# A threshold search of a sparse layer: level and count in one tile, one predicated copy per bracket end, both masks from one instruction, the level as a ninth candidate, no negated level

## The reference, cut to what matters

```python
z = x_flat @ ternary_quant(W_syn).T + b_syn          # [2048, 1024]
k = max(1, int(N * (1.0 - TARGET_SPARSITY)))         # 102
topv, _ = jax.lax.top_k(z, k)
thresh = topv[:, -1:]                                # the 102nd largest of each token
hidden = jnp.where(z >= thresh, jax.nn.relu(z), 0.0)
out = hidden @ ternary_quant(W_out).T + b_out
return layernorm(x + out, gamma, beta)
```

## Time and profile before

| | |
|---|---|
| time, median of 3 runs | 1194.39 us (1192.79 to 1199.39) |
| time of the profiled execution | 1195.06 us |
| its span, first to last instruction | 1193.3 us |
| busy in the span | PE 91%, PEld 62%, DVE 76%, ACT 52%, POOL 18% |
| granted TensorE clock, mean | 0.962 |

### The profile page before, as it was taken

One profiled execution on the slowest core, in us unless ns is written; L12 is line 12 of the kernel. 1 busy time (PEld: TensorE's weight loads), 2 busy tenths in 40 slices (PEclk: granted clock), 3 DMA queues, 4 the chain that ended last, 5 costly groups with the idle time before them and its releaser, 6 DMA issues. The chain is left out here.

```text
span 1193.3 us, 18401 instructions
## 1 busy us (share of the span) xinstructions
PE 1084.1 (91%) x7046; PEld 745.7 (62%) x7046; DVE 904.9 (76%) x1698; ACT 625.9 (52%) x1096; POOL 216.0 (18%) x176
## 2 busy tenths in 40 slices
PE   8889999999999989777867889999997899999998
PEld 8623333333333437566757768888886698989976
DVE  7689999999999634689888886555553878798853
ACT  5338787887887764776641233333333433433343
POOL 1308100000000002000034203000000744554410
...
GB/s 198 235 133 55 17 40 54 24 34 55 31 26 2 2 1 32 1 1 1 11 9 1 1 93 33 21 36 19 36 1 50 14 1 1 1 1 1 1 67 5
DMA packets 25290, 40.02 MB, mean 34 GB/s; under 512 B 3560, under 2 KB 12784, under 8 KB 25200
## 3 DMA queue, kind: packets, MB, share of 16 engines
...
...
q10 hardware_dynamic: 576, 0.00, 0.0%
...
## 5 line engine op out<-in xcount | busy, mean ns | idle before, releaser
L771 DVE TENSOR_REDUCE att_mx<-att_ps_m 128x2 f32<-128x1024 f32 x256 | 310.9, 1224 | 23.6 <-PE att_ps_m L637 19.9
L748 ACT ACTIVATE att_prob<-att_ps_s 128x512 f32<-128x512 f32 x512 | 278.2, 596 | 88.5 <-PE att_ps_s L687 76.5
L703 PE MATMUL att_ps_o<-att_prob,v_rows 128*32 128x256 f32 (+1 forms) x1920 | 159.3, 405 | 0.0
L1980 POOL TENSOR_TENSOR qry_prod<-qry_qr,lin_ksum 128x512 f32<-128x512 f32 x64 | 92.9, 1451 | 303.7 <-ACT qry_qr L2102 289.6
L687 PE MATMUL att_ps_s<-qst,kst 50*128 50x512 f32 x512 | 128.0, 496 | 11.0 <-ACT att_prob L748 10.4
L687 PEld LDWEIGHTS att_ps_s<-qst,kst 50*128 50x128 f32 x512 | 48.0, 183 | 123.8 <-ACT att_prob L748 114.2
L637 PE MATMUL att_ps_m<-kst,qst 48*128 48x512 f32 x512 | 109.9, 424 | 8.8 <-DVE att_mx L771 7.2
L2102 ACT ACTIVATE qry_qr<-qry_ps_q 128x512 f32<-128x512 f32 x64 | 38.3, 598 | 132.8 <-PE qry_ps_q L153 124.0
L153 PE MATMUL qry_ps_o<-qry_m,qry_n_hi 128*128 128x256 f32 x512 | 99.5, 293 | 0.5 <-DVE qry_n_lo L2010 0.5
L703 PEld LDWEIGHTS att_ps_o<-att_prob,v_rows 128*32 128x32 f32 x1920 | 38.1, 108 | 84.7 <-ACT att_prob L748 71.1
L1692 DVE SCALAR_TENSOR_TENSOR key_k_lo<-kf_ps,key_k_hi 128x512 fp32r<-128x512 f32 x64 | 44.2, 691 | 61.6 <-ACT key_k_hi L1770 61.0
...
## 6 DMA issues: line engine op xcount, KB each, us to landing
...
```

The costliest lines, as they stand in the source:

```text
L703: ins = nc.tensor.matmul(ps_o[32 * h:32 * h + 32, cols], vall[:, NS * b + s, h0 + h, :], prob[:, u % PR, h, cols], start=s == 0, stop=s == ...
L748: nc.scalar.activation(prob[:, u % PR, 2 * j + r, :], ps_s[:, (n + r) % BANKS, :], ACT.Exp).then_inc(exp_ok, 1)
L771: nc.vector.reduce_max(mx[:, v % 2, :, m], ps_m[:, n % 2], AX.X).then_inc(m_rd, 1)
L1980: nc.gpsimd.tensor_tensor(prod[:, u % 2, :], qr[:, u % 2, :], ksum[:, b, cols(n)], ALU.mult).then_inc(pr_ok, 1)
```

## The change

`lev` and `cnt` become the two halves of one tile `now`, and the four bracket arrays become one tile `ends` (side, level or count, tile), so that one predicated copy of 128x8 moves a level and its count. Both masks come out of one `scalar_tensor_tensor` against a constant tile `below_end` of ones and zeros. `square` and `missed` lose their waits. The two bracket widths are one subtraction. The Sign activation gets scale -1 and the level itself as bias, so `nlev` goes, in `first_level` too. The bracket's first ends are computed from mean and deviation and not from the level. In `threshold` the level is put in front of the eight as a ninth candidate, the counts are compared with a constant tile `place`, and the flag is reduced first. `settle` writes the integer flag in one instruction. On POOL there are two more small memsets at the start of the stage, on DVE one more instruction on `place` in step 0.

```diff
--- before.py
+++ after.py
@@ -879,21 +879,23 @@
...
-        lev = st.sb("lev", [P, d.NT])
-        nlev = st.sb("nlev", [P, d.NT])
+        now = st.sb("now", [P, d.NC, 2, TPC])
         sgn = st.sb("sgn", [P, d.NT])
-        cnt = st.sb("cnt", [P, d.NT])
-        lo, hi, clo, chi = (st.sb(n, [P, d.NT]) for n in ("lo", "hi", "clo", "chi"))
+        ends = st.sb("ends", [P, 2, 2, TPC])
+        width = st.sb("width", [P, 2, TPC])
+        below_end = st.sb("below_end", [P, 2, TPC])
         missed = st.sb("missed", [P, d.NT])
-        t1, t2, t3, msk = (st.sb(n, [P, TPC]) for n in ("t1", "t2", "t3", "msk"))
+        t1, t2, t3 = (st.sb(n, [P, TPC]) for n in ("t1", "t2", "t3"))
+        msk = st.sb("msk", [P, 2, TPC])
+        doubt = st.sb("doubt", [P, 2 * TPC])
...
-        top = st.sb("top", [P, d.NT, 8])
-        pick = st.sb("pick", [P, TPC, 8])
-        iota8 = st.sb("iota8", [P, 8])
-        iota_i = st.sb("iota_i", [P, 8], mybir.dt.int32)
+        top = st.sb("top", [P, d.NT, 9])
+        pick = st.sb("pick", [P, TPC, 9])
+        place = st.sb("place", [P, 9])
+        iota_i = st.sb("iota_i", [P, 9], mybir.dt.int32)
         thr = st.sb("thr", [P, d.NT])
         flag = st.sb("flag", [P, 2])
         flag_i = st.sb("flag_i", [P, 1], mybir.dt.int32)
@@ -963,7 +965,9 @@
             def _(pool):
                 link = chain(pool, gp)
                 link(nc.gpsimd.memset(ones[:], 1.0))
-                link(nc.gpsimd.iota(iota_i[:], pattern=[[1, 8]], base=0, channel_multiplier=0))
+                link(nc.gpsimd.iota(iota_i[:], pattern=[[1, 9]], base=0, channel_multiplier=0))
+                link(nc.gpsimd.memset(below_end[:, 0, :], 1.0))
+                link(nc.gpsimd.memset(below_end[:, 1, :], 0.0))
                 nc.gpsimd.memset(as_f32(share[:]), 1.0 / P).then_inc(on, 1)
                 pool.wait_ge(w_in[2], 48)
                 for s in range(d.NC + DEPTH - 1):
@@ -1035,90 +1039,83 @@
                 def first_level(c):
                     cs = slice(TPC * c, TPC * (c + 1))
                     dve.wait_ge(zroot, c + 1)
-                    link(nc.vector.scalar_tensor_tensor(out=lev[:, cs], in0=zsd[:, cs], scalar=SPREAD0,
-                                                        in1=zmv[:, :, 0], op0=ALU.mult, op1=ALU.add))
-                    nc.vector.tensor_scalar(nlev[:, cs], lev[:, cs], -1.0, None, ALU.mult).then_inc(lev_ok, 1)
-                    nc.vector.scalar_tensor_tensor(out=lo[:, cs], in0=zsd[:, cs], scalar=-0.6, in1=lev[:, cs],
-                                                   op0=ALU.mult, op1=ALU.add)
-                    nc.vector.scalar_tensor_tensor(out=hi[:, cs], in0=zsd[:, cs], scalar=0.6, in1=lev[:, cs],
-                                                   op0=ALU.mult, op1=ALU.add)
-                    nc.vector.memset(clo[:, cs], 122.0)
-                    link(nc.vector.memset(chi[:, cs], -68.0))
+                    nc.vector.scalar_tensor_tensor(out=now[:, c, 0, :], in0=zsd[:, cs], scalar=SPREAD0,
+                                                   in1=zmv[:, :, 0], op0=ALU.mult, op1=ALU.add).then_inc(lev_ok, 1)
+                    for side, (off, count) in enumerate(((-0.6, 122.0), (0.6, -68.0))):
+                        nc.vector.scalar_tensor_tensor(out=ends[:, side, 0, :], in0=zsd[:, cs], scalar=SPREAD0 + off,
+                                                       in1=zmv[:, :, 0], op0=ALU.mult, op1=ALU.add)
+                        ins = nc.vector.memset(ends[:, side, 1, :], count)
+                    link(ins)
 
                 def next_level(c, r):
 
                     cs = slice(TPC * c, TPC * (c + 1))
-                    LEV, CNT = lev[:, cs], cnt[:, cs]
+                    LEV, CNT = now[:, c, 0, :], now[:, c, 1, :]
                     dve.wait_ge(cnt_ok, TPC * (ROUNDS * c + r + 1))
-                    link(nc.vector.tensor_scalar(CNT, sgn[:, cs], 0.5, d.N / 2 - AIM, ALU.mult, ALU.add))
-
-                    link(nc.vector.tensor_tensor(t1[:], CNT, CNT, ALU.mult))
-                    link(nc.vector.tensor_scalar(missed[:, cs], t1[:], 16.5, None, ALU.is_gt))
+                    link(nc.vector.tensor_scalar(CNT, sgn[:, cs], -0.5, d.N / 2 - AIM, ALU.mult, ALU.add))
+                    square = nc.vector.tensor_tensor(t2[:], CNT, CNT, ALU.mult)
                     if r == ROUNDS - 1:
+                        link(square)
+                        link(nc.vector.tensor_scalar(missed[:, cs], t2[:], 16.5, None, ALU.is_gt))
                         return
-                    m = msk[:].bitcast(U32)
-                    link(nc.vector.tensor_scalar(msk[:], CNT, 0.0, None, ALU.is_gt))
-                    nc.vector.copy_predicated(lo[:, cs], m, LEV)
-                    link(nc.vector.copy_predicated(clo[:, cs], m, CNT))
-                    link(nc.vector.tensor_scalar(msk[:], CNT, 0.0, None, ALU.is_le))
-                    nc.vector.copy_predicated(hi[:, cs], m, LEV)
-                    link(nc.vector.copy_predicated(chi[:, cs], m, CNT))
+
+                    both = [P, 2, TPC]
+                    link(nc.vector.scalar_tensor_tensor(out=msk[:], in0=CNT.unsqueeze(1).to_broadcast(both), scalar=0.0,
+                                                        in1=below_end[:], op0=ALU.is_gt, op1=ALU.is_equal))
+                    nc.vector.tensor_scalar(missed[:, cs], t2[:], 16.5, None, ALU.is_gt)
+                    for side in range(2):
+                        ins = nc.vector.copy_predicated(ends[:, side],
+                                                        msk[:, side].bitcast(U32).unsqueeze(1).to_broadcast(both),
+                                                        now[:, c])
                     if r == 0:
                         link(nc.vector.scalar_tensor_tensor(out=t1[:], in0=CNT, scalar=1.0 / SLOPE, in1=zsd[:, cs],
                                                             op0=ALU.mult, op1=ALU.mult))
                         link(nc.vector.tensor_tensor(t1[:], t1[:], LEV, ALU.add))
                     else:
-                        nc.vector.tensor_tensor(t1[:], clo[:, cs], chi[:, cs], ALU.subtract)
-                        link(nc.vector.tensor_tensor(t2[:], hi[:, cs], lo[:, cs], ALU.subtract))
-                        nc.vector.reciprocal(t3[:], t1[:])
-                        link(nc.vector.tensor_tensor(t2[:], t2[:], clo[:, cs], ALU.mult))
+                        link(ins)
+                        link(nc.vector.tensor_tensor(width[:], ends[:, 0], ends[:, 1], ALU.subtract))
+                        nc.vector.reciprocal(t3[:], width[:, 1, :])
+                        link(nc.vector.tensor_tensor(t2[:], width[:, 0, :], ends[:, 0, 1, :], ALU.mult))
                         link(nc.vector.tensor_tensor(t2[:], t2[:], t3[:], ALU.mult))
-                        link(nc.vector.tensor_tensor(t1[:], t2[:], lo[:, cs], ALU.add))
-                    link(nc.vector.copy_predicated(LEV, missed[:, cs].bitcast(U32), t1[:]))
-                    nc.vector.tensor_scalar(nlev[:, cs], LEV, -1.0, None, ALU.mult).then_inc(lev_ok, 1)
+                        link(nc.vector.tensor_tensor(t1[:], ends[:, 0, 0, :], t2[:], ALU.subtract))
+                    nc.vector.copy_predicated(LEV, missed[:, cs].bitcast(U32), t1[:]).then_inc(lev_ok, 1)
 
                 def eight(c, js):
 
                     for j in js:
                         t = TPC * c + j
                         ins = nc.vector.scalar_tensor_tensor(out=below[:, t % 2, :], in0=z_tile(t),
...
-                        ins = nc.vector.max(top[:, t, :], below[:, t % 2, :])
+                        ins = nc.vector.max(top[:, t, 1:9], below[:, t % 2, :])
                     link(ins)
 
                 def threshold(c):
 
                     cs = slice(TPC * c, TPC * (c + 1))
-                    LEV, THR = lev[:, cs], thr[:, cs]
-
-                    link(nc.vector.tensor_scalar(t1[:], cnt[:, cs], -1.0, KEEP - 1 - AIM, ALU.mult, ALU.add))
-                    nc.vector.tensor_scalar(t2[:], t1[:], -1.0, None, ALU.is_equal)
-                    link(nc.vector.tensor_tensor(pick[:], t1[:].unsqueeze(2).to_broadcast([P, TPC, 8]),
-                                                 iota8[:].unsqueeze(1).to_broadcast([P, TPC, 8]), ALU.is_equal))
-                    nc.vector.tensor_tensor(t2[:], t2[:], LEV, ALU.mult)
+                    LEV, CNT, THR = now[:, c, 0, :], now[:, c, 1, :], thr[:, cs]
+
+                    nc.vector.scalar_tensor_tensor(out=doubt[:, 0:TPC], in0=LEV, scalar=0.0, in1=missed[:, cs],
+                                                   op0=ALU.is_le, op1=ALU.max)
+                    link(nc.vector.tensor_tensor(doubt[:, TPC:], top[:, cs, 1], LEV, ALU.is_equal))
+                    nc.vector.reduce_max(flag[:, 0:1], doubt[:], AX.X).then_inc(flag_ok, 1)
+                    nc.vector.tensor_copy(top[:, cs, 0], LEV)
+                    link(nc.vector.tensor_tensor(pick[:], CNT.unsqueeze(2).to_broadcast([P, TPC, 9]),
```

(20 more changed lines are left out.)

2 lines of the change are left out of this document (1 added, 1 removed).

## The result

The kernel after takes 1188.44 us (median of 7 runs, 1184.93 to 1190.45), the kernel before beside it 1196.19 us (7 runs, 1192.79 to 1199.56). The ratio is 0.9929, 95% interval [0.9914, 0.9944]: 0.7% faster, 8.5 us by the ratio and 7.75 by the medians. A second timing on another chip gave 0.9923 [0.9902, 0.9944]. The forecast was 1183.5 in a range of 1178.5 to 1188.5. The median lies inside that range by 0.06 us only, and that is luck: the forecast started from a before of 1194.39 us, and before took 1196.19 us in this timing. The ratio applied to 1194.39 gives 1185.9. The direction came as forecast and the interval excludes no change; the gain is 8.5 us by the ratio, with an interval of 6.7 to 10.3, where the sum had 10.9.

The account below looks back on a forecast made before the run. No engine was taken as full throughout: DVE bounds steps 2, 4 and 5, PE step 3. Terms 1.24 + 4.2 + 0 + 3.4 + 3.4 - 1.35 = 10.9 us saved gave 1183.5 us, range 1178.5 to 1188.5.

Parts of the forecast that it names:

- The price of a small instruction: On DVE, a 128x4 instruction counts 0.20 us from start to start with a wait, 0.08 without.
- Steps 0 and 1: Start of the stage: chunk 0's level and `xt_lo` come sooner, 1.24 us saved; extra instructions in step 0 covered by waits.
- Step 2: Stretch to 544 us, bound by DVE: shorter rounds, `threshold`, `settle` and `first_level` save 4.2 us together.
- Step 3: Stretch to 587 us, bound by PE: nothing gained, DVE's savings go into its wait for PE.
- The marker of 5.4 us for the transposes: Sign to look for: PE's transposes of step 3 start some 5.4 us sooner.
- Step 4: DVE-bound stretch after step 3: rounds save 1.04, 0.96 and 1.2 us, `settle` 0.20, together 3.4.
- Step 5: DVE-bound stretch to 657 us: `threshold` of chunk 3 saves 3.2 us, `settle` 0.20, together 3.4.
- Step 6: Last step: early flag matmul leaves PE idle, transposes run at half clock, DVE waits; a cost of 1.35 us.
- B: Steps 4 and 5: holding by POOL stays, wide copies cost more; only 6.5 us saved, 1187.9 us; chance 0.17.
- C: Step 3: TensorE's clock stays up after a shorter pause, 2.2 us more saved, 1180 us; chance 0.12.
- D: Step 2: ScalarE's rounds or PE bind too; only 2 to 4 us saved, 1191 us; chance 0.07.
- E: In `settle`: one token without settled threshold triggers the slow search, 133 us, giving 1317 us; chance 0.04.

Follow-up runs that it names:

- Experiment 5: The changed kernel with the left-out waits put back in the rounds, the merged instructions kept; 1187.55 us, a single run.
- Experiment 7: The changed kernel with five more linked 128x4 copies in each of chunk 1's three rounds; 1189.05 us, ratio 0.9938 to before.
- experiment 6: The changed kernel with five more linked 128x4 copies in each of chunk 2's three rounds; 1186.9 us, ratio 0.9912 to before.
- experiment 1: The kernel before with only the new `first_level` and `next_level`, old `threshold` and `settle` kept; 1189.33 us, ratio 0.9939 to before.
- experiment 2: The kernel before with only the new `threshold` and `settle`, old rounds kept; 1192.25 us, ratio 0.9968 to before.
- experiment 8: The kernel before with POOL's weight subtraction issued one step later; 1197.55 us, a single run, against 1197.21 beside it.
- experiment 9: The changed kernel with 15 and not 6 useless matmuls ahead of the masked rows in steps 5 and 6; 1184.88 us, ratio 0.9913 to before.
- experiment 10: The kernel of experiment 9 with also 20 and not 9 useless matmuls ahead of chunk 3's turn; 1178.96 us, ratio 0.9852 to before.

## Why the prediction was right, and where its size was off

- **The price of a small instruction: right.** 0.20 us from start to start with a wait, 0.08 without; the wide copies and the mask cost no more than the narrow ones, as assumed. Three numbers fell within 0.05 us: 1.77, 1.18 and 1.08 against 1.80, 1.20 and 1.04. ScalarE's Sign with scale -1 takes as long in both kernels, 1.13 to 1.14 us in the median, as assumed. Experiment 5 shows the wait itself as the cause.
- **Steps 0 and 1: right.** 1.24 was forecast. The first two profiles differ by 1.7, but that holds TensorE's clock; without PE's two long groups step 1 is 1.25 shorter. The round r = 0 of chunk 0 lost 1.06 in the traces. With the old rounds all else in step 1 takes 18.13 to 18.15 in four profiles, with the new ones 16.88 to 16.91 in nine, and 17.41 with the waits put back.
- **Step 2: right.** 4.2 forecast, 4.36 measured. The held round r = 0 of chunk 1 gave 1.10 and not 0.9 (3.56 to 2.46). Experiment 7 shows the step follows DVE us for us.
- **Step 3: right.** Nothing, and experiment 6 shows that at least 2.5 of 3.0 us of DVE work disappear in it. The marker of 5.4 us for the transposes was not met as written: they start 2.6 us earlier on the span's own clock. The work ahead of the stage ended 3.5 us later in this profile, and steps 0 to 2 gave 6.1; counted from the start of the stage they are 6.1 earlier.
- **Step 4: right in kind, 0.7 too large.** 3.4 forecast, 2.71 measured; this is the term that was mis-sized. The rounds gave 1.05, 0.99 and 1.21. But the masking pass of `eight` (L1087, two of 128x1024) now falls beside POOL's adds more fully and takes 3.44 us, 2.95 before. That is the contention moved to the neighbour; the sum had looked for it only in the small instructions. Of these 0.49 us 0.28 come back, since the later start shortens the third round (0.93 saved in experiment 1, 1.21 here), so that its 1.2 was met by luck. The wait for ScalarE ahead of the first round grew by 0.18 (0.50 to 0.68), and two evacuations ahead of the masking pass (L1132) by 0.10.
- **Step 5: right, two errors that cancel.** `threshold(3)` gave 3.87 and not 3.2: two instructions are held in full, 0.62 at 641.81 (L1105) and 0.60 at 642.56 (L1108), and not four groups. POOL's subtraction then held L115 for 0.45. Together 3.61 with the 0.2 of `settle`, against 3.4, so the sum is luck. Experiments 1, 2 and 8 show the instruction held for 2.27 us, and that it goes with the threshold's merging or with the move of POOL's work.
- **Step 6: right.** A cost of 1.41, 1.35 forecast, from the two waits foretold; experiment 9 takes both away by filling the pause.
- **The Trainium skill, SBUF — State Buffer, section "SBUF: two separate sides"**, which gives VectorE and GpSimd one exclusive lock, agrees with the rows in which a small instruction waits 0.6 us, or 2.27, for one of POOL. That each instruction would be held singly is not what they show: with 0.15 us the mask, with its two inputs in SBUF, went through behind a held one.

Of the rivals, B (the holding stays) did not occur: `threshold(3)` ended 1.02 us ahead, and a wide copy cost nothing more; the third round of step 4 still ran beside POOL's adds for 3.9 of its 4.4 us, which gave more than that rival's 0.6. C did not occur by itself (the pause before step 3's transposes shrank to 5.87 and not to 4 us), but was built in experiment 10. D is refuted by step 2. E did not occur: no row of the slow search is in the trace.

**The whole.** With the clock of steps 0 and 1 left out, the steps give 10.5 us in the first profiles and 10.0 in the means. In the first profiles step 4 is 0.7 short of the sum, and steps 2 and 5 give 0.4 more than it. The two timings give 8.5 us (6.7 to 10.3) and 9.2 (6.7 to 11.7), so up to 2 us may be missing outside the steps, or nothing. The last sentence of the sum, "all that follows moves rigidly", is neither shown nor refuted. In two profiles of before and three of after the part ahead of the stretch is 0.9 us longer (448.2 and 449.1) and the part behind it 1.7 (503.1 and 504.8), although nothing was changed there. But the spread is larger than that: within after's three profiles ahead is 447.5 to 451.1, and behind 504.2 to 506.0, and before's two are 501.8 and 504.4 behind. Over all nine profiles with after's rounds and threshold, the experiments' among them, the part ahead is 449.1 and the part behind 503.9, against 449.2 and 503.1 in three of before's kind, which leaves 0.7. Whether that is an effect of the change or spread stays open. One profile of after took 1183.14 us, the forecast to 0.4 us; the two others took 1189.
